# Two idle PSUM banks join the ring of row maxima and scores, and half of one addition moves behind a mask, in an attention and feed-forward kernel

## What is computed

```python
x = x + layernorm(attention(layernorm(x)))
x = x + layernorm(ffn(layernorm(x)))
# attention: 16 heads of 32; kqv = x @ Wqkv + bqkv
scores = einsum('bsnh,btnh->bnst', k, q) / sqrt(32)   # key rows, query columns
scores = triu(scores) - 10000 * tril(ones, -1)        # a key sees only its own and later queries
attn = softmax(scores, axis=2)                        # over the keys
out = einsum('bnkq,bknh->bqnh', attn, v) @ Wo + bo
# ffn: integer weights, dequantised; down(silu(gate) * up), inner width 2048
```

## Time and profile before

| | |
|---|---|
| median of three runs | 1763.86 us |
| the profiled execution | 1762.82 us |
| its span in the trace | 1761.1 us |
| PE busy | 1595.6 us, 91% |
| DVE busy | 955.1 us, 54% |
| ACT busy | 744.4 us, 42% |
| POOL busy | 594.4 us, 34% |
| granted TensorE clock, mean | 0.966 of full |

### The profile page before, as it was taken

One profiled execution on the slowest core, in us unless ns is written; L12 is line 12 of the kernel. 1 busy time (PEld: TensorE's weight loads), 2 busy tenths in 40 slices (PEclk: granted clock), 3 DMA queues, 4 the chain that ended last, 5 costly groups with the idle time before them and its releaser, 6 DMA issues.

```text
span 1761.1 us, 24904 instructions
## 1 busy us (share of the span) xinstructions
PE 1595.6 (91%) x9631; PEld 673.7 (38%) x9632; DVE 955.1 (54%) x1785; ACT 744.4 (42%) x1207; POOL 594.4 (34%) x814
## 2 busy tenths in 40 slices
PE   2478999999899998999997779999999999999997
PEld 1233433344333333443343224444444444444443
DVE  3475666576776677755776423355434343434254
ACT  4414655466665467555664443333222222222221
POOL 2204455555664567455754662011000000000000
PEclk9889999999999999999998779999999999999998
DMA  6201121123221213220222443112111111111000
GB/s 200 69 11 26 49 61 30 32 79 91 61 61 49 55 61 90 61 61 15 77 82 83 154 143 108 37 66 84 36 36 37 37 42 33 40 54 41 8 25 25
DMA packets 59464, 106.25 MB, mean 60 GB/s; under 512 B 11473, under 2 KB 11473, under 8 KB 59089
## 3 DMA queue, kind: packets, MB, share of 16 engines
q1 hardware_dynamic: 59344, 104.66, 19.4%
HBM read 54.02 MB, written 25.17 MB: 45 GB/s over the span
## 4 chain that ended last, share of the span: by engine, by line
PE 69%; DVE 11%; POOL 7%; ACT 6%; issue 4%; DMA 1%; ACTq 0%; DVEq 0%; POOLq 0%
PE ps L805 24%; PE ps L728 15%; PE ps L822 12%; PE ps L789 10%; DVE mcol L1033 5%; PE ps L765 4%; ACT pt L909 4%; POOL pt L1217 4%; PE ps L741 2%; DVE st L936 1%; PE ps L749 1%; PE ps L695 1%; DMA xin<-in_x 1%; POOL rs L1164 1%; POOL pt L1207 1%
## 5 line engine op out<-in xcount | busy, mean ns | idle before, releaser
L909 ACT ACTIVATE pt<-ps,nrm 128x512 f32<-128x512 f32 (+1 forms) x640 | 361.9, 646 | 396.0 <-PE ps L765 383.7
L805 PE MATMUL ps<-x2in,gu 128*128 128x512 f16 x2048 | 462.6, 379 | 0.0
L1033 DVE TENSOR_REDUCE mcol<-ps 128x1 f32<-128x512 f32 (+3 forms) x768 | 370.4, 549 | 103.7 <-PE ps L749 76.1
L805 PEld LDWEIGHTS ps<-x2in,gu 128*128 128x128 f16 x2048 | 200.3, 98 | 239.8 <-issue 0.2
L1161 POOL TENSOR_SCALAR rs<-mv 128x1 f32<-128x1 f32 x128 | 26.2, 205 | 684.0 <-DVE mv L940 678.2
L1108 DVE SCALAR_TENSOR_TENSOR hf<-ps,usc,sg 128x512 f32<-128x512 f32 x128 | 96.1, 751 | 264.0 <-PE ps L805 252.0
L1217 POOL TENSOR_TENSOR pt<-pt 128x1024 f32<-128x1024 f32 x96 | 225.1, 2373 | 5.0 <-ACT pt L909 4.5
L765 PE MATMUL ps<-qpack,kpack 98*128 98x512 f16 (+3 forms) x768 | 180.8, 343 | 26.3 <-DVE mcol L1033 24.5
L822 PE MATMUL ps<-wd,hh 128*128 128x512 f16 x512 | 194.0, 379 | 0.0
L822 PE MATMUL ps<-wd,hl 128*128 128x512 f16 x512 | 194.0, 379 | 0.0
L925 ACT ACTIVATE hh<-hf 128x512 f16<-128x512 f32 x128 | 80.7, 630 | 260.1 <-DVE hf L1108 246.5
(11 more groups left out here) (110 smaller groups left out, 1598.2 us busy)
## 6 DMA issues: line engine op xcount, KB each, us to landing
qpack<-stage SPq DMA_DIRECT2D x192, 64.0 KB, 2.0
kpack<-stage SPq DMA_DIRECT2D x192, 64.0 KB, 2.0
xin<-in_x SPq DMA_DIRECT2D x32, 256.0 KB, 2.8
xr<-in_x SPq DMA_DIRECT2D x32, 256.0 KB, 2.8
x1d<-xr SPq DMA_DIRECT2D x32, 256.0 KB, 2.2
x2d<-x2s SPq DMA_DIRECT2D x32, 256.0 KB, 2.0
x2in<-x2d SPq DMA_DIRECT2D x8, 1024.0 KB, 5.5
x1in<-x1d SPq DMA_DIRECT2D x8, 1024.0 KB, 5.8
```

Source lines behind the costliest of these rows:

```text
L805: mm = pe.matmul(bk, GU[:, c, m, i * 128:(i + 1) * 128], x2in[:, 1 - k, :, p, c, :], start=p == 0 and c == 0, stop=p == 1 and c == 3)
L909: act.activation(Pt[:, PBUF[step], h, off:512], ps[:, BANK[job], off:512], ACT.Exp, scale=esc).then_inc(s_ex, 1)
L1033: mm = dve.tensor_reduce(mcol[:, n % 2, col:col + 1], ps[:, BANK["max", n, i, h], at:at + w], AX.X, ALU.max)
```

## The change

PLAN gets a marker `step` at each step, and `sum` becomes a job of one half (0 or 2). In step 7 the half 2 stands behind the scores, and so behind the masks, on POOL. Where ACT waits for an addition it waits for the half that holds its head. The counter becomes a list, `RING`: bank 5 joins at a step without a projection and leaves at the next marker; bank 7 joins at the invert of the first half and leaves at `den` (1,4), which like `den` (0,0) now takes bank 7 by the same rule as any other use and waits for its former user. The feed-forward part keeps its ring of four.

```diff
@@ order_of_jobs
         for s, (j, kb) in enumerate(STEPS):
             here = rows.get(NS * n + s, [])
+            add(("step", n, s))
...
                 if summed and pend[2] > 0:
-                    add(("sum",) + pend)
+                    add(("sum",) + pend + (0,))
+                    if s != 7:
+                        add(("sum",) + pend + (2,))
                 if s == NS - 1:
                     add(("den", n, 1, 0))
             plan += [("score", n, j, kb, h) for h in range(4)]
+            if s == 7:
+                add(("sum",) + pend + (2,))
@@ banks
     elif kind == "mjob":
         if not attention:
-            attention, turn = True, 0
+            attention, RING = True, [0, 1, 2, 3, 4]
         uses = [("max",) + job[1:] + (h,) for h in range(4)]
+    elif kind == "step":
+        if 5 in RING:
+            RING.remove(5)
+        if job[2] not in projections(job[1]):
+            RING.append(5)
+        continue
+    elif kind == "invert":
+        held[7] = job
+        if job[2] == 0:
+            RING.append(7)
+        continue
+    elif kind == "den":
+        if job[2:] == (1, 4):
+            RING.remove(7)
+        if job[2:] in ((0, 0), (1, 4)):
+            take(job, 7)
+        continue
...
     for use in uses:
-        take(use, turn % (4 if feed else 5 if attention else 6))
-        turn += 1
+        take(use, RING[0])
+        RING.append(RING.pop(0))
@@ PE, den
-                        if kb == 4 * j and (n, j) != (0, 0):
-                            e.wait_ge(s_dt, 2 * n + j)
+                        if kb == 4 * j:
+                            bank(job)
                         if kb < 4 * j:
-                            e.wait_ge(s_sum, 2 * NO["sum", n, 1, 3])
+                            e.wait_ge(s_sum, NO["sum", n, 1, 3, 2])
@@ ACT, score
-                            e.wait_ge(s_sum, 2 * NO[("sum", before[0]) + STEPS[before[1]]])
+                            e.wait_ge(s_sum, NO[("sum", before[0]) + STEPS[before[1]] + (h // 2 * 2,)])
@@ POOL, sum
-                    n, j, kb = a
+                    n, j, kb, h = a
                     e.wait_ge(s_num, STEP[n, 1, 0])
-                    for h in (0, 2):
-                        e.wait_ge(s_ex, NO["score", n, j, kb, h + 1])
-                        if kb > 1:
-                            e.wait_ge(s_sum, 2 * NO[job] - 3 + h // 2)
-                        pool.tensor_tensor(Pt[:, 2, h:h + 2, :], Pt[:, 2, h:h + 2, :], Pt[:, PBUF[STEP[a]], h:h + 2, :],
-                                           ALU.add).then_inc(s_sum, 1)
+                    e.wait_ge(s_ex, NO["score", n, j, kb, h + 1])
+                    if kb > 1:
+                        e.wait_ge(s_sum, NO["sum", n, j, kb - 1, h])
+                    pool.tensor_tensor(Pt[:, 2, h:h + 2, :], Pt[:, 2, h:h + 2, :], Pt[:, PBUF[STEP[a[:3]]], h:h + 2, :],
+                                       ALU.add).then_inc(s_sum, 1)
```

More of the change, by code:

```diff
@@ L295 @@
 BANK, FORMER, held = {}, {}, {}
-turn, attention, feed = 0, False, False
+RING, attention, feed = [0, 1, 2, 3, 4, 5], False, False
 def take(use, bank):
@@ L308 @@
         if not feed:
-            feed, turn, LEFT = True, 0, dict(held)
+            feed, RING, LEFT = True, [0, 1, 2, 3], dict(held)
         uses = [("gate", job[1]), ("up", job[1])]
@@ L503, in emptied @@
             return {"ln1_turn": s_xl, "turn2": s_x2l, "norms": s_cmax, "qk": s_tq, "vproj": s_vw,
-                    "mturn": s_mf, "score": s_ex, "woproj": s_yt}[kind], NO[use]
+                    "mturn": s_mf, "score": s_ex, "woproj": s_yt, "invert": s_dt}[kind], NO[use]
         def used(no):
```

## The result

The changed kernel takes 1741.34 us (median of four runs, 1740.20 to 1743.19) against 1762.36 us for the kernel before: a ratio of 0.988, 95% interval 0.9859 to 0.9901, 21 us faster. 1737 was forecast, in a range of 1719 to 1758. In the changed kernel the lines of PE, ACT and DVE stand 24 further down, those of POOL mostly too: `den` and `num` are L813, scores L789, max L765 and L773, transposes L719, the reduction L1057, the mask L1231, the addition L1240.

The account below looks back on a forecast made before the run. PE was taken to bound attention, busy 93% of the time, so its idle time could be won. The terms 18 + 21.7 - 13.4 = 26.3 us off the profiled 1762.8 gave 1736.5, so 1737 us, range 1719 to 1758.

Parts of the forecast that it names:

- Part 1: Half of POOL's addition goes behind the mask, so PE's den starts earlier, in groups 3, 7, 11, 13, 15: 18 us.
- Rival (d): In group 3 the exponentials of (1,4) come late and the mask moves little: 12 of 18 us go, 1749 us; 8%.
- Part 2: A deeper ring in steps 4 to 7 cuts PE's bank waits: 20 us, with 1.7 us of clock 21.7.
- 34.5 have a bank free early enough: Of 41.7 us of PE's bank waits, 34.5 would find a bank free in the new ring; the upper end.
- down from 44.5 to some 12 us: Sign expected: PE's waits on ring banks held by DVE or ACT fall from 44.5 to some 12 us.
- The 14.5 us taken off the 34.5: Deductions from the ring's gain: 4 us for mask waits, 7 for num behind exponentials, 3.5 for DVE sometimes behind.
- The 7 us taken off: In steps 5 and 7 num can't come sooner than ACT's exponentials allow: some 0.4 us lost in each of 16 groups.
- The 1.7 us of clock at 229 us: Low clock in group 1, following ring waits, was to go with the deeper ring: 1.7 us won.
- Rival (b): The ring wins only 4 us, its waits turning into ones on exponentials or DVE's reductions: 1755 us; 15%.
- Part 3: In nine groups den (1,4) waits for a reduction holding bank 7: 10.0 us lost, with clock 13.4.
- Rival (a): The new wait at step 8 decides, with low clock behind it in nine groups: 51 us lost, 1775 us; 8%.
- rival (c): More is won: the new wait's stalls are paid back by shorter waits, the ring gives 34: 1718 us; 12%.

Follow-up runs that it names:

- E2: The changed kernel without the new ring: old ring of five banks, only the half addition moved and ACT's waits on halves; 1740.0 us.
- E9: The kernel before with only the second half of the last addition moved behind the masks; old ring, ACT waits for whole additions; 1743.7 us.
- E7: The changed kernel, but ACT waits for both halves of an addition before it writes any head; 1739.7 us.
- E1: The changed kernel, but bank 7 leaves the ring at the start of step 8, not at den (1,4); 1725.4 us.
- E10: The kernel before with the new ring only, bank 7 leaving at the start of step 8; addition not moved, whole waits; 1757.3 us.
- E4: The changed kernel with bank 5 alone joining the ring and bank 7 kept for den; 1740.0 us.
- E5: E1, but bank 5 stays with the projections, so only bank 7 joins the ring; 1726.6 us.
- E6: E1 with both halves of the last addition behind the masks in all groups; 1731.6 us.
- E12: E6 with DVE's join of the row maxima made a reduction with one SBUF input; 1720.3 us.
- E8: The changed kernel with one more wait: before den (1,4) PE waits for the reduction of step 8's last max head; 1757.2 us.

## Why the prediction was right, step by step

**Part 1, the half addition: 18 us forecast.** Right. Groups 3, 7 and 11 were to get 12.8 us shorter together; they got 5.0, 3.9 and 3.9 shorter, in the change and in E2 alike. Counted from the group's first score the masks of group 3 end 39.9 us on, in place of 42.2. Group 13 got 3.1 us shorter (3.0 forecast), group 15 3.4 (2.4); in E2 it is 4.9 and 6.8, so these two sizes agree in part by luck. The move alone gives 19 us (E9), with half waits 21 (E2). By the forecast's terms that is 21: the 18, and the 1.1 us of groups 4, 8 and 12, which part 3 gave away again. The clock behind group 3 is 1.00, as said. The gap left is 1.10 us, not 0.6: with the ring PE is there earlier. Rival (d) is out. That the wait for single halves "is what makes the mask's input timely in group 3" was wrong: E7 does without it, and its `den` waits 1.12 us there.

**Part 2, the ring: 21.7 us forecast, 14.6 measured** (E2 to E1, the medians; each is known to some 2 or 3 us). This is the term that was mis-sized. The step that failed: "34.5 have a bank free early enough". It held every use at the time it had in the old trace. The waits fell by 15 us, not by 34.5: "down from 44.5 to some 12 us" was to be seen, and 29.7 are left. The 14.5 us taken off the 34.5 were not enough. Of the 25.0 us in E1 17 stand in steps 4 to 7, where the ring has its six or seven banks. That PE, coming earlier, reaches the next bank before DVE or ACT has emptied it fits these rows, but no use was followed one by one. The 7 us taken off because `num` would wait for the exponentials don't show: `num` and `den` wait 0.4 us for ACT in two waits, before and after. The 1.7 us of clock at 229 us are not the ring's (E2, E9, E10). Bank 5, which the forecast counted beside bank 7, is worth nothing that can be measured (E4, E5). And the ring's worth hangs on the move: without it some 5 us (E10). Rival (b), with 4 us for the ring, holds only where the addition isn't moved, and there the time goes to the mask, not to the exponentials of `num`.

**Part 3, the new wait: 13.4 us forecast, 15.9 measured** (E1 to the change, the medians; 14.8 by the ratios). Right in place and size. Losses of 2.3, 2.0, 1.5, 0.7 and 1.55 us were forecast in groups 1, 2, 4, 5 and 6 (in group 4 the 1.10 us that isn't won and 0.4); the gaps are 2.10, 1.88, 1.41, 0.70 and 1.41. Group 9 has 1.37 in place of 0.7: its four reductions begin only when DVE is through with an operation of 0.72 us. The 15.9 hold the 3.3 us not won in groups 4, 8 and 12, which the 13.4 don't; like with like it is 16.7 forecast. Two falls of the clock were forecast, behind groups 1 and 2; one came, in group 2, and in E7, with the same gaps, one in group 1. The number of falls was a guess that came out half. Rival (a) would have needed 4.4 us a group; rival (c), that the gaps are paid back, is out by E1.

The sum was 26.3 us, or 21.3 + 21.7 - 16.7 with the 3.3 us counted in part 1 and taken off in part 3. The experiments give 21 + 14.6 - 15.9 = 19.8, and the change itself measured 21. In the profiles attention got 24.1 us shorter. So the 5.3 us that are missing are those of part 2, 7.1 too much; part 1 and part 3 were right to about 1 us, which is closer than the medians are known.

## What to carry to other kernels

A bank lent out by an accumulator must come back a step before it is wanted: lent up to the last moment it cost here 16 us and used up all that the longer ring had won. Waits counted off an old trace are an upper end, as the engine that gets rid of one may meet the next; here 43% of what had looked removable went, and it turned into time only once the other engine's chain had been made shorter (E10 against E1). Where an operation is moved past another, look at what runs beside it at its new place, not only at what waits for it.

## What the runs showed of the hardware

A small DVE operation with two inputs in SBUF doesn't run beside POOL's addition. `mjoin` takes 0.165 us alone; beside the addition it lasts until that ends, 2.12 us in group 2 of E6, and PE waited 9.2 us for it over nine groups. As a reduction with one input it took 0.177 us beside the same additions (E12). The Trainium skill, "SBUF — State Buffer", section "Who interferes with whom", says that a VectorE instruction with two SBUF inputs contends with a GpSimd one that reads SBUF, and that a reduction doesn't. The traces agree, with 2.12 us for the one and 0.177 for the other. It need not cost anything: in the changed kernel the join takes 769 ns on average, and PE never waits for it in attention. In the kernel before it cost little too: the join was held by the addition in groups 3, 7, 11 and 13, for 0.07 to 0.8 us, and for 0.25 us in seven others, where it ended with POOL's subtraction L1200.

The clock: with PE idle before `den` for 2.86 or 2.87 us the granted clock was at the low level of 1.2 GHz behind it in groups 3, 7 and 11 of the kernel before. Idle for 3.39 us, it fell in groups 7 and 11 of E10 and stayed at 1.00 in group 3. Idle for 1.9 to 2.15 us with the clock at 1.00 before, it fell in six of thirteen groups (E8). It never fell at 1.10 us, in groups 3, 7 and 11 of the changed kernel and 4, 8 and 12 of the kernel before. And the same two gaps were followed by low clock the other way round in the change and in E7. So whether a single gap of 1.9 to 3.4 us costs the clock isn't told by its length, and one execution doesn't settle it.
